# Six recurrent layers: the last table row loaded in two parts, two loads on each other's queue, and another order of VectorE's first steps

## What is computed

```python
n_layers = ih.shape[0]                      # 6
for i in range(n_layers):
    gate = ih[i][token]                     # 1024 tokens, table of 4000 rows
    state = jnp.tanh(state + jnp.matmul(state, hh[i]) * gate)
return state                                # 1024 x 256
```

## Time and profile before

| | us |
|---|---|
| median of 3 runs | 59.74 |
| lowest and highest | 59.72, 60.28 |
| the profiled execution | 59.85 |
| its span, first to last instruction | 58.0 |

### The profile page before, as it was taken

How to read it: one execution, slowest core, us unless ns; L and a number is a source line. 1 busy time by engine, 2 the same in 40 slices (tenths; PEclk the granted TensorE clock), 3 DMA queues, 4 the chain that set the end, 5 groups by cost and what they waited for, 6 DMA issues and landing times.

```text
span 58.0 us, 872 instructions
## 1 busy us (share of the span) xinstructions
PE 51.1 (88%) x280; PEld 44.1 (76%) x280; DVE 39.7 (68%) x62; ACT 40.1 (69%) x71; POOL 35.5 (61%) x35
## 2 busy tenths in 40 slices
PE   0959999999999799999999999999999999999000
PEld 0749988898687789888888988889888898888000
DVE  1216997999956858385958907999089990899700
ACT  0710899922407489899499999779997799844800
POOL 2077057676605389989936996289862997714500
PEclk9999999999999999999999999999999999999998
DMA  0698975322365560000000000000000000004482
GB/s 0 90 283 246 217 224 189 94 60 55 86 223 180 162 205 15 0 0 0 0 0 0 0 0 0 0 6 0 0 6 0 11 0 0 0 0 181 186 268 89
DMA packets 5668, 4.46 MB, mean 77 GB/s; under 512 B 2218, under 2 KB 5290, under 8 KB 5664
## 3 DMA queue, kind: packets, MB, share of 16 engines
q1 hardware_dynamic: 3456, 3.41, 18.6%
q0 software_dynamic: 1152, 0.73, 5.4%
q10 hardware_dynamic: 1056, 0.27, 2.1%
HBM read 8.92 MB, written 1.05 MB: 172 GB/s over the span
## 4 chain that ended last, share of the span: by engine, by line
PE 49%; issue 11%; DMA 11%; ACT 8%; POOL 8%; DVE 4%; POOLq 1%; ACTq 1%; DVEq 0%
PE prod L520 17%; PE turned L501 9%; PE prod L529 9%; DMA gate<-gates_dram,row_of 6%; PE prod L474 6%; POOL gate L247 6%; DMA last_row<-gates_dram 5%; PE turned L542 5%; PE turned L483 4%; POOL sl L263 2%; ACT s L323 2%; ACT gate L297 2%; ACT gate_t L316 1%; POOLq L192 1%; DVE prod L409 1%
## 5 line engine op out<-in xcount | busy, mean ns | idle before, releaser
L263 POOL TENSOR_TENSOR sl<-s,sh 128x512 fp32r<-128x512 f32 x12 | 15.4, 1294 | 6.0 <-ACT s L323 5.8
L520 PE MATMUL prod<-sh,wr 128*128 128x512 f32 (+1 forms) x68 | 17.9, 384 | 0.0
L474 PE MATMUL prod<-w,s 128*128 128x256 f32 x64 | 14.8, 379 | 0.0
L409 DVE TENSOR_TENSOR prod<-prod,gate_t 128x512 f32<-128x512 f32 x14 | 9.8, 700 | 6.6 <-PE prod L529 6.6
L520 PEld LDWEIGHTS prod<-sh,wr 128*128 128x128 f32 x68 | 12.1, 188 | 2.1
L474 PEld LDWEIGHTS prod<-w,s 128*128 128x128 f32 x64 | 11.8, 192 | 1.3
L247 POOL DMA_INDIRECT gate<-gates_dram,row_of x8 | 8.1, 1009 | 6.0 <-ACT gate L297 2.2
L529 PE MATMUL prod<-sl,wr 128*128 128x512 f32 (+1 forms) x34 | 10.1, 377 | 0.0
L414 DVE TENSOR_TENSOR pre<-prod,s 128x512 f32<-128x512 f32 x14 | 9.7, 691 | 0.5
L323 ACT ACTIVATE s<-pre 128x512 f32<-128x512 f32 x14 | 8.7, 622 | 1.1 <-DVE pre L414 1.1
L316 ACT COPY gate_t<-turned 128x512 f32<-128x512 f32 x16 | 8.6, 586 | 1.1 <-PE turned L501 1.1
(11 more groups left out here) (31 smaller groups left out, 32.6 us busy)
## 6 DMA issues: line engine op xcount, KB each, us to landing
w<-hh_dram SPq DMA_DIRECT2D x5, 256.0 KB, 2.8
s<-state_t_dram SPq DMA_DIRECT2D x4, 256.0 KB, 3.2
out_t_dram<-s SPq DMA_DIRECT2D x2, 256.0 KB, 2.1
out_t_dram<-s SPq DMA_DIRECT2D x4, 128.0 KB, 1.9
w<-hh_dram ACTq DMA_DIRECT2D x1, 256.0 KB
gate<-gates_dram,row_of POOLq DMA_INDIRECT x8, 3.6
last_row<-gates_dram ACTq DMA_DIRECT2D x1, 6.0 KB, 2.9
tok<-token_dram SPq DMA_DIRECT2D x1, 4.0 KB, 1.6
```

The lines of the kernel that those rows point to most:

```text
L263: nc.gpsimd.tensor_tensor(of_unit(sl[:, l % 2], h, c), of_unit(s, h, c), of_unit(sh[:, l % 2], h, c).bitcast(f32), ALU.subtract).then_inc( ...
L409: nc.vector.tensor_tensor(prod_bank[u][:, :], prod_bank[u][:, :], gate_t[:, l % 2, u], ALU.mult).then_inc(unit_gated[u], 1)
L474: last = nc.tensor.matmul(prod[q][:, t, :], of_quarter(s, q)[:, c, t * P:(t + 1) * P], w[:, l, c, :], start=c == 0, stop=c == KC - 1)
L520: nc.tensor.matmul(bank, wr[:, l, k, half, c * P:(c + 1) * P], of_unit(sh[:, (l - 1) % 2], h, k)[:, tokens], start=half == 0 and k == 0, s ...
```

## The change

The load of `last_row` is cut in two DMAs, both issued by ACT: layers 0 and 1 (128 x 2 x 2 values) and then layers 2 to 5. TensorE waits for the first part ahead of piece one of the spread and for the second ahead of pieces two and three. Layer 0's weights are issued by SP in the place of state quarter 1, and quarter 1 by ACT, as its third DMA. TensorE's warm-up has five transposes instead of six. On DVE all four fills stand ahead of the first patch. gating(2) stands directly behind gating(1), ahead of sum_up(1), and patch(2) behind sum_up(1).

```diff
-WARM_UP = 6
+WARM_UP = 5
@@ semaphores
-        row_in = sem("row_in")
+        first_piece_in = sem("first_piece_in")
+        pieces_in = sem("pieces_in")
@@ SP
                 sp.dma_start(tok[:, :], token).then_inc(tok_in, 16)
                 load_state(0)
-                load_state(1)
+                load_weights(0)
                 sp.wait_ge(state_in[0], 16)
                 load_state(2)
                 sp.wait_ge(w_in[0], 16)
@@ ACT
-                act.dma_start(last_row[:, :, :], last_row_v).then_inc(row_in, 16)
-                act.dma_start(w[:, 0], w_v[0]).then_inc(w_in[0], 16)
+                act.dma_start(last_row[:, 0:PIECE, :], last_row_v[:, 0:PIECE, :]).then_inc(first_piece_in, 16)
+                act.dma_start(last_row[:, PIECE:LAYERS, :], last_row_v[:, PIECE:LAYERS, :]).then_inc(pieces_in, 16)
+                act.dma_start(of_quarter(s, 1), state_v[1]).then_inc(state_in[1], 16)
@@ DVE
-                for i, t, count in DVE_FILLS[:3]:
+                for i, t, count in DVE_FILLS:
                     fill(i, t, count)
                 dve.wait_ge(index_step, 3)
                 patch(0, 0, 1)
-                for i, t, count in DVE_FILLS[3:]:
-                    fill(i, t, count)
                 patch(0, 1, 1)
                 gating(0)
                 patch(1, 0, len(EARLY_TILES))
                 sum_up(0)
                 gating(1)
+                gating(2)
+                sum_up(1)
                 patch(2, 0, len(EARLY_TILES))
-                sum_up(1)
-                gating(2)
                 gating(4)
                 sum_up(2)
                 gating(3)
@@ PE
-                pe.wait_ge(row_in, 16)
                 for i in range(PIECES):
+                    if i == 0:
+                        pe.wait_ge(first_piece_in, 16)
+                    else:
+                        pe.wait_ge(pieces_in, 16)
```

## The result

| | before | changed |
|---|---|---|
| median | 59.88 | 61.31 |
| lowest and highest | 59.72, 60.28 (4 runs) | 61.16, 61.54 (4 runs) |
| the profiled execution | 59.85 | 61.16 |
| its span | 58.0 | 59.4 |
| start of turn(3), "T" | 19.17 | 20.48 |

The ratio is 1.023, with a 95% interval of 1.017 to 1.030: slower, though whether by more than 2% is not settled. Ratios and their intervals leave out every run that is over 1.5% above the fastest of its kernel, while medians take in all runs, so the two need not agree. Beside the later experiments the changed kernel was timed once more: 61.15 against 59.80, ratio 1.021 (1.013 to 1.029). I had forecast 59.5 with a range of 58.9 to 60.3, so the time is outside the range and on the other side of no change.

The account below looks back on a forecast made before the run. The start of turn(3), behind gathers and then unbroken TensorE work, was taken to bound the kernel. Gathers -0.67, gating(2)'s wait +0.45, warm-up, queues and fills 0: -0.22, from median 59.74 to 59.5, range 58.9 to 60.3.

Parts of the forecast that it names:

- Where it is read: At the start of turn(3), 19.17 before: a us off there is a us off the end.
- Landing of the second part, taken at 3.9: Last row's second DMA, issued by ACT at 1.22: lands at 3.6 to 4.2, bounds 3.1 to 5.4; gathers 0.67 earlier.
- My upper bound, 5.4: Latest landing of the second part, from layer 0's weights, issued in this slot before and landed by 5.44.
- my rule: Shift of ACT's fills and every gather behind them: 4.57 less the second part's landing, at most 1.0.
- TensorE's pace: TensorE's clock at the lower level ahead of about 6.3: work there costs double, an earlier start gives back half.
- TensorE's own bound for T: Start of turn(3) that TensorE alone would allow: about 18.1 after the change, lower than the bound by tile 5.
- Gating(2) ahead of sum_up(1), 0.45: On DVE, gating(2) waits for tile 5 with later steps behind it, which takes 0.45 from the gain.
- Queues and fills at nothing: The two loads that change queues, and fills moved ahead of copies on DVE: each claimed to cost zero.
- The slower one: Rival: second part served behind the state, landing from 4.7 on; 0.6 slower, at 5.0 0.9 slower, 60.6; chance 0.17.
- L: The landing time of the last row's second part, taken at 3.9.
- The rule of the Trainium skill: Rival: DMAs of all queues interleave, second part lands at 3.3 or so; gain 0.55, time 59.2; chance 0.15.

Follow-up runs that it names:

- the second profile: The changed kernel timed once more beside other experiments, nothing changed: median 61.15 (six runs), profiled execution 61.42.
- the clearest pair: Changed kernel with second part issued by SP ahead of state and old order of sums, without and with four transposes in the spread's pause: 61.27 and 59.83.
- The swap: Kernel before with layer 0's weights on SP and state quarter 1 on ACT, nothing else: 59.69, 59.74, 61.35 and 61.53, median 60.55.
- both causes are out: Changed kernel with the old order of the sums and five more transposes in the pause of the spread: 60.08, ratio 1.004.
- the parts swapped: Changed kernel with ACT issuing the part of layers 2 to 5 first and that of layers 0 and 1 second: 61.58, one run.
- the run with the parts alone: Changed kernel with SP and ACT issuing state and weights only once both parts of the last row have landed: 63.02, one run.
- With one load alone: Changed kernel with the last row in one load, and state and weights issued only once it has landed: 62.76, one run.

## Why the prediction was wrong

**Where it is read.** Right. T decides, and behind it TensorE runs without a break.

**Landing of the second part, taken at 3.9.** Wrong by 1.0: 4.90. The slot was read rightly: first packets after 3.15. The step that failed is "then come its packets, 0.1 to 0.4". They took from 3.4 to 4.4, with the rest of quarter 0 and layer 0's weights beside them in q1, and landed half a us behind that. My upper bound, 5.4 from the weights in this slot, held it; the reason for staying near the lower end, that small packets need little of an engine, did not. The shift was -0.33 by my rule and -0.46 at the gathers.

**TensorE's pace.** This is the larger fault over all runs, though not in the first profile, where tile 5 set T. I wrote that what runs ahead of about 6.3 costs double, and took that moment as fixed. So TensorE's own bound for T stood at 18.1 and no longer came into the sum. By my own numbers the change put a pause into the spread, from 3.6 to 3.95, and I never asked what it would do to the clock; it came as 1.2, from about 3.7 to 4.95. In its place: plain(0) to plain(2) at 6.28 and 7.38 in two executions instead of 5.35, which puts turn(0) at 12.84 and 13.82, 1.35 and 2.3 later than before (0.4 and 0.3 of it from the later start of plain(0)). In the second profile this sets T; filling the pause took 1.4 off in the clearest pair.

**Gating(2) ahead of sum_up(1), 0.45.** Right in mechanism, and in size as far as the runs tell. Alone it cost 0.57 by the medians (0.4 to 1.1 by the ratio's interval, so 0.45 is at its low end), and in its profile T came 0.19 later though the gathers came 0.21 earlier, which makes 0.40. The chain from gating(2) to T is 4.41 in both kernels that have this order. In the changed kernel tile 5 came 0.4 later after its issue than I had taken: gating(2) starts 3.64 behind it, 3.19 in the run with this order alone.

**Queues and fills at nothing.** The swap costs nothing in the trace that shows it, but two of its four runs stay unexplained, so zero is not shown for its median. The fills, the patch order and the warm-up were not tried by themselves; all that is left when both causes are out is 0.3, and it holds the late gathers too.

**The rivals.** The slower one, with L over 4.7 and gating(2) behind it, had the right place and 0.17 of the chances. It gives T = 19.62 + 0.33 = 19.95 for the L that came, 0.8 us slower; the other 0.5 of the first profile is 0.13 at the gathers and 0.4 at tile 5. Neither it nor any other rival had TensorE's clock in it, and that is what set T in the second profile (61.42). The rule of the Trainium skill that I weighed against the row (DMA: Bandwidth & Descriptors, Issuing engines are not separate DMA queues) would have put the landing at 3.3. The trace stands against the use that I made of it: the second part did share the engines with the large loads, from 3.4 on, and landed at 4.90.

## What to carry to other kernels

A small load that many things wait for should be the first in its queue and whole; a second part of it, issued half a us later, stood in line with the large loads and came 1.2 later than the whole (4.90 against 3.66). Where a wait is put into the start of TensorE's work, price it twice, as time and as a delay of its clock, and fill it with transposes that write to a bank not yet in use. An instruction moved ahead of others on an in-order engine waits for its latest operand, and all behind it wait too: gating(2) had its product long before, but not its gates.

## What the runs showed of the hardware

TensorE's clock costs the plain steps of this kernel from nothing to 2.0 us (5.35 to 7.38 for the same 24 matmuls). In six profiled executions with a pause inside the spread (0.4 to 1.1 by the rows) they took 5.92 to 7.38. In nine with no pause there they took 5.35 to 6.07, and 7.03 in one of them; among these are the parts swapped, with 1.84 of idle time ahead of the whole spread, at 5.65. So the two groups overlap in time per execution, and it is the pair of kernels with and without four transposes that shows the effect of the pause.

In the run with the parts alone the clock was lost again, and there the granted clock shows it (tenths, in 40 slices of 1.5 us):

```profile
PEclk9999996579999999999999999999999999999999
```

TensorE was busy from 1.58 to 5.6 and then idle for 2.8. plain(0) began at 8.39 at the full pace, 0.22 from matmul to matmul. The granted clock fell to 0.50 at about 9.7, while TensorE was at work, and rose again at about 13.1; the 24 matmuls took 7.13. With one load alone (2.5 of idle time) it fell at 8.8 and rose at 12.2, with 7.13 as well.

The Trainium skill, TensorE: Matmul & The Clock Gate, section Part 1: The HAM clock gate, gives the cost of the ramp as under 1% of a typical kernel span; by it nothing here would be worth counting. The measured cost is up to 2.0 us in the plain steps, and 1.44 us, 2.4%, at the end of the kernel in the clearest pair, and here the measurement decides.

Before the rise TensorE had run nothing but transposes in the kernel before (plain steps at 5.35), and little else in the two kernels with the old order of the sums and the pause filled (5.50 and 5.60). What made the clock rise late in single executions without a pause stays open.
